# A fused GNN layer: the n gate summed in a PSUM bank that VectorE filled, and half of the edge scaling on VectorE

## The reference

```python
h = jnp.maximum(_layernorm(x), 0.0)
msg_input = jnp.concatenate([h[src], h[dst]], axis=1)
for t in range(4):
    m = jax.nn.relu(msg_input @ W1[t] + b1[t]) @ W2[t] + b2[t]
    msgs = msgs + jnp.where((edge_type == t)[:, None], m, 0)
agg = jax.ops.segment_sum(msgs, dst, num_segments=num_nodes)
gi = agg @ W_ih.T + b_ih                 # i_r, i_z, i_n
gh = h @ W_hh.T + b_hh                   # h_r, h_z, h_n
r = sigmoid(i_r + h_r); z = sigmoid(i_z + h_z)
n = tanh(i_n + r * h_n)
out = x + (1.0 - z) * n + z * h
```

## Time and profile before

| | |
|---|---|
| median of three runs | 1849.3 us (1848.07 to 1853.45) |
| span of the profiled execution | 1849.7 us |
| PE busy, weight loads | 1666.5 us (90%), 1413.8 us (76%) |
| VectorE busy | 1709.9 us (92%) |
| ScalarE busy | 1504.8 us (81%) |
| GpSimd busy | 1178.7 us (64%) |
| HBM traffic over the span | 172 GB/s |
| granted TensorE clock | 1.00 in all stretches of 200 us between 200 and 1600 us |

### The profile page before, as it was taken

One profiled execution on the slowest core, in us unless ns is written; L12 is line 12 of the kernel. 1 busy time (PEld: TensorE's weight loads), 2 busy tenths in 40 slices (PEclk: granted clock), 3 DMA queues, 4 the chain that ended last, 5 costly groups with the idle time before them and its releaser, 6 DMA issues.

```text
span 1849.7 us, 43490 instructions
## 1 busy us (share of the span) xinstructions
PE 1666.5 (90%) x10181; PEld 1413.8 (76%) x10181; DVE 1709.9 (92%) x4382; ACT 1504.8 (81%) x3401; POOL 1178.7 (64%) x1982
## 2 busy tenths in 40 slices
PE   0126899999999999999999999999999999999998
PEld 0125788888888888888888888888888888888786
DVE  8596799999999999999999999999999999999887
ACT  0025788898888888888889898889898889898895
POOL 4777776776776776767765656566566566666420
PEclk9999899999999999999999999999999999999999
DMA  2225677677777777777776776776767777776643
GB/s 69 51 51 139 171 191 195 186 193 191 192 185 192 189 193 185 185 192 187 188 187 190 187 190 181 193 186 187 185 191 183 190 183 191 186 189 185 174 137 94
DMA packets 477072, 319.73 MB, mean 173 GB/s; under 512 B 106705, under 2 KB 463009, under 8 KB 476962
## 3 DMA queue, kind: packets, MB, share of 16 engines
q10 hardware_dynamic: 261792, 156.12, 28.2%
q1 hardware_dynamic: 185730, 106.99, 25.1%
q0 software_dynamic: 29440, 55.47, 11.6%
HBM read 211.65 MB, written 106.72 MB: 172 GB/s over the span
## 4 chain that ended last, share of the span: by engine, by line
PE 55%; ACT 8%; issue 5%; ACTq 4%; DVE 1%; DVEq 0%
PE bank L1333 12%; PE bank L1335 9%; PE bank L1334 9%; PE bank L1413 8%; PE bank L1403 4%; PE bank L1395 4%; ACT n_zc L1288 3%; ACT n_h L1200 2%; PE bank L1425 2%; PE bank L1442 2%; PE bank L1424 2%; PE bank L1452 2%; ACTq L1217 2%; ACT e_r L1276 2%; ACTq L1238 2%
## 5 line engine op out<-in xcount | busy, mean ns | idle before, releaser
L581 POOL DMA_INDIRECT e_x<-in_x,rows_now x816 | 799.2, 979 | 243.3 <-issue 230.6
L1183 ACT ACTIVATE e_h<-e_x,shift,rstd 128x128 f32<-128x128 f32 x816 | 354.8, 490 | 93.7 <-DVE shift L1049 93.7
L1200 ACT ACTIVATE n_h<-n_x,shift,rstd 128x128 f32<-128x128 f32 x784 | 361.4, 488 | 2.2 <-issue 2.2
L1333 PE MATMUL bank<-n_h_hi,whh_hi 128*128 128x512 f32 x588 | 263.5, 448 | 37.5 <-ACT n_zc L1288 29.1
L1333 PE MATMUL bank<-n_a_hi,wih_hi 128*128 128x512 f32 x588 | 248.9, 423 | 0.0
L1072 DVE TENSOR_SCALAR n_sel<-iota,n_rel 128x256 fp32r<-128x256 f32 x784 | 237.3, 364 | 7.1 <-POOL n_rel L632 7.1
L1413 PE MATMUL bank<-n_sel,n_win 128*128 128x256 f32 x1568 | 234.9, 292 | 8.5 <-DVE n_sel L1072 8.3
L1335 PE MATMUL bank<-n_a_hi,wih_lo 128*128 128x512 f32 x588 | 232.3, 395 | 0.0
L1335 PE MATMUL bank<-n_h_hi,whh_lo 128*128 128x512 f32 x588 | 232.2, 395 | 0.0
L1334 PE MATMUL bank<-n_h_lo,whh_hi 128*128 128x512 f32 x588 | 232.0, 395 | 0.0
L1334 PE MATMUL bank<-n_a_lo,wih_hi 128*128 128x512 f32 x588 | 232.0, 394 | 0.0
(11 more groups left out here) (178 smaller groups left out, 4022.8 us busy)
## 6 DMA issues: line engine op xcount, KB each, us to landing
n_win<-messages SPq DMA_DIRECT2D x1568, 64.2 KB
messages<-e_msg ACTq DMA_DIRECT2D x204, 257.0 KB, 2.4
n_x<-in_x ACTq DMA_DIRECT2D x195, 256.0 KB
out<-n_out ACTq DMA_DIRECT2D x195, 256.0 KB
e_x<-in_x,rows_now POOLq DMA_INDIRECT x816
rows_now<-lists SPq DMA_DIRECT2D x204, 2.0 KB
lists<-picks,list_rows POOLq DMA_INDIRECT x72
w<-in_W SPq DMA_DIRECT2D x1, 512.0 KB, 4.8
```

Of the source, the lines that this page charges most:

```text
L581: G.indirect_dma_start(e_x[:, s, 2 * end + t, :], None, x, bass.IndirectOffsetOnAxis(ap=rows_now[:, s, t, end:end + 1], axis=0)).then_inc( ...
L1183: last = A.activation(e_h[:, s % 2, k, :], e_x[:, s, k, :], ACT.Relu, scale=rstd[:, slot, col + k:col + k + 1], bias=shift[:, slot, col + ...
L1200: last = A.activation(n_h[:, s % 2, cols], n_x[:, s, cols], ACT.Relu, scale=rstd[:, slot, col + 4 + k:col + 5 + k], bias=shift[:, slot, co ...
L1333: T.matmul(o, w_hi, v_hi, start=start, stop=False)
```

## The change

Four edits. VectorE's `(h_n + b) * r` is written into PSUM bank BIN instead of `n_t`, and PE's three products of the n gate add onto it, without clearing the bank first; so the products wait for n_ted, ScalarE's tanh reads the bank after n_gate_in, and the add of line 1105 with its semaphore is gone. One matmul ahead of the loop writes BIN once. VectorE makes tiles 2 and 3 of e_h (`scale_edges`, in the place of the add), as scale and shift without ReLU, and gives a new semaphore e_scaled. ScalarE makes tiles 0 and 1 with Relu as before, and its copy of the transposed tiles becomes a Relu. GpSimd waits for e_scaled wherever it waits for e_normed, and so does PE. ScalarE's order: n_h tile 0 goes ahead of sigmoid r, the tanh ahead of n_h tiles 1 and 2.

```diff
@@ -362,6 +362,7 @@
         n_stats = sem("n_stats")
         e_tagged = sem("e_tagged")
         e_normed = sem("e_normed")
+        e_scaled = sem("e_scaled")
         e_turned = sem("e_turned")
         e_evaced = sem("e_evaced")
         e_hid = sem("e_hid")
@@ -391,7 +392,6 @@
         n_red = sem("n_red")
         n_zed = sem("n_zed")
         n_ted = sem("n_ted")
-        n_ued = sem("n_ued")
         n_ned = sem("n_ned")
         n_ded = sem("n_ded")
         n_eed = sem("n_eed")
@@ -654,6 +654,7 @@
                         linked(G.tensor_tensor(new[:], root_t[:], old[:], ALU.mult))
                 if due(first - 4):
                     pool.wait_ge(e_normed, first - 4)
+                    pool.wait_ge(e_scaled, first - 4)
                 if due(first - LAG + 5):
                     pool.wait_ge(n_normed, first - LAG + 5)
                 G.tensor_tensor(rstd[:, slot, :], root_t[:], root[:], ALU.mult).then_inc(ln_rooted, 4)
@@ -670,6 +671,7 @@
                     pool.wait_ge(l_loaded[m % UNROLL], uses(i, m % UNROLL, UNROLL, 16))
                     if due(i - 7):
                         pool.wait_ge(e_normed, i - 7)
+                        pool.wait_ge(e_scaled, i - 7)
                 if h is not None:
                     wait_half(h)
                 transfers_may_start(i + 1 + 2 * TYPES)
@@ -1049,6 +1051,20 @@
                     V.scalar_tensor_tensor(out=shift[:, slot, :], in0=bn[:, slot, :, 1], scalar=-1.0, in1=rstd[:, slot, :],
                                            op0=ALU.mult, op1=ALU.mult).then_inc(ln_shifted, 4)
 
+            def scale_edges(i, m):
+
+                q, s, third = i - 7, (m - 7) % UNROLL, (m - 7) % 4
+                if not within(q, UNITS):
+                    return
+                dve.wait_ge(ln_shifted, q - third + 4)
+                if due(q - 1):
+                    dve.wait_ge(e_turned, q - 1)
+                for k in (2, 3):
+                    col = 8 * third + k
+                    last = V.tensor_scalar(e_h[:, s % 2, k, :], e_x[:, s, k, :], rstd[:, s // 4, col:col + 1],
+                                           shift[:, s // 4, col:col + 1], ALU.mult, ALU.add)
+                last.then_inc(e_scaled, 1)
+
             def step(i, m):
                 g, s = i - LAG - 2, (m - LAG - 2) % 4
                 if within(g, NG):
@@ -1079,9 +1095,9 @@
                 if within(g, NG):
                     dve.wait_ge(n_red, g + 1)
                     dve.wait_ge(n_gate_hn, g + 1)
-                    if due(g - 1):
-                        dve.wait_ge(n_ned, g - 1)
-                    V.scalar_tensor_tensor(out=n_t[:, s, :], in0=bank[BHN][:], scalar=bhh[:, 2:3], in1=n_r[:, s, :],
+                    if due(g):
+                        dve.wait_ge(n_ned, g)
+                    V.scalar_tensor_tensor(out=bank[BIN][:], in0=bank[BHN][:], scalar=bhh[:, 2:3], in1=n_r[:, s, :],
                                            op0=ALU.add, op1=ALU.mult).then_inc(n_ted, 1)
                 ln_part(i, m, 2)
                 g, s = i - LAG + 1, (m - LAG + 1) % UNROLL
@@ -1098,11 +1114,7 @@
                     dve.wait_ge(n_ahi, g + 1)
                     V.tensor_tensor(n_a_lo[:, s % 2, :], bank[BA][:], n_a_hi[:, s % 2, :].bitcast(F32),
                                     ALU.subtract).then_inc(n_alo, 1)
-                g, s = i - LAG, (m - LAG) % 2
-                if within(g, NG):
-                    dve.wait_ge(n_gate_in, g + 1)
-                    dve.wait_ge(n_ted, g + 1)
-                    V.tensor_tensor(n_t[:, s, :], bank[BIN][:], n_t[:, s, :], ALU.add).then_inc(n_ued, 1)
+                scale_edges(i, m)
                 if within(i - LAG + 8, NG):
                     last = node_stats(i - LAG + 8, m - LAG + 8, m - 1)
                 if last is not None:
@@ -1177,13 +1189,12 @@
                 if not within(q, UNITS):
                     return
                 slot, col = wait_norm(i, m)
-                if 0 in tiles and due(q - 1):
+                if due(q - 1):
                     act.wait_ge(e_turned, q - 1)
                 for k in tiles:
                     last = A.activation(e_h[:, s % 2, k, :], e_x[:, s, k, :], ACT.Relu,
                                         scale=rstd[:, slot, col + k:col + k + 1], bias=shift[:, slot, col + k:col + k + 1])
-                if 3 in tiles:
-                    last.then_inc(e_normed, 1)
+                last.then_inc(e_normed, 1)
 
             def normalise_nodes(i, m, tiles):
                 g, s = i - LAG + 2, (m - LAG + 2) % UNROLL
@@ -1239,21 +1250,21 @@
                                   n_out[:, s, :].rearrange("p (k d) -> p k d", k=TILES)).then_inc(n_stored[s], 16)
 
             def step(i, m):
-                normalise_edges(i, m, (0, 1, 2))
+                normalise_edges(i, m, (0, 1))
+                normalise_nodes(i, m, (0,))
                 g, s = i - LAG, (m - LAG) % 2
                 if within(g, NG):
                     act.wait_ge(n_gate_r, g + 1)
                     if due(g - 1):
                         act.wait_ge(n_ted, g - 1)
                     A.activation(n_r[:, s, :], bank[BRZ][:], ACT.Sigmoid, bias=bsum[:, 0:1]).then_inc(n_red, 1)
-                normalise_edges(i, m, (3,))
                 store_messages(i, m)
                 q, s = i - 8, (m - 8) % 2
                 if within(q, UNITS):
                     act.wait_ge(e_turned, q + 1)
                     if due(q - 1):
                         act.wait_ge(e_hid, q - 1)
-                    A.activation(e_ht[:, s, :], bank[BE0][:], ACT.Copy).then_inc(e_evaced, 1)
+                    A.activation(e_ht[:, s, :], bank[BE0][:], ACT.Relu).then_inc(e_evaced, 1)
                 g, s = i - LAG + 1, (m - LAG + 1) % 2
                 if within(g, NG):
                     act.wait_ge(n_turned, g + 1)
@@ -1262,7 +1273,6 @@
                     A.activation(n_h_hi[:, s, :], bank[BT[s]][:], ACT.Copy).then_inc(n_hhi, 1)
                     act.wait_ge(n_summed, g + 1)
                     A.activation(n_a_hi[:, s, :], bank[BA][:], ACT.Copy).then_inc(n_ahi, 1)
-                normalise_nodes(i, m, (0,))
                 store_out(i, m)
                 load_x(i, m)
                 q, s = i - 9, (m - 9) % 2
@@ -1275,13 +1285,14 @@
                         kind = 2 * ((m - 9) % 2) + t
                         last = A.activation(e_r[:, s, cols], bank[BE1][:, cols], ACT.Relu, bias=b1_cols[:, kind:kind + 1])
                     last.then_inc(e_relued, 1)
-                normalise_nodes(i, m, (1, 2))
                 g, s = i - LAG, (m - LAG) % 2
                 if within(g, NG):
-                    act.wait_ge(n_ued, g + 1)
+                    act.wait_ge(n_gate_in, g + 1)
                     if due(g - 1):
                         act.wait_ge(n_ded, g - 1)
-                    A.activation(n_n[:, s, :], n_t[:, s, :], ACT.Tanh, bias=bih[:, 2:3]).then_inc(n_ned, 1)
+                    A.activation(n_n[:, s, :], bank[BIN][:], ACT.Tanh, bias=bih[:, 2:3]).then_inc(n_ned, 1)
+                normalise_nodes(i, m, (1, 2))
+                if within(g, NG):
                     act.wait_ge(n_gate_z, g + 1)
                     if due(g - 1):
                         act.wait_ge(n_eed, g - 1)
@@ -1328,19 +1339,21 @@
                      ).then_inc(s_ranked, 1)
             pe.wait_ge(s_edges_ready, 1)
             pe.wait_ge(s_gates_ready, 1)
-
-            def product(o, w_hi, w_lo, v_hi, v_lo, start, stop):
-                T.matmul(o, w_hi, v_hi, start=start, stop=False)
-                T.matmul(o, w_hi, v_lo, start=False, stop=False)
-                return T.matmul(o, w_lo, v_hi, start=False, stop=stop)
-
-            def gate(b, row, s, sources):
+            T.matmul(bank[BIN][:], ones_r[:], b2_rows[:], start=True, stop=True)
+
+            def product(o, w_hi, w_lo, v_hi, v_lo, start, stop, onto):
+                start = start and not onto
+                T.matmul(o, w_hi, v_hi, start=start, stop=False, skip_group_check=onto)
+                T.matmul(o, w_hi, v_lo, start=False, stop=False, skip_group_check=onto)
+                return T.matmul(o, w_lo, v_hi, start=False, stop=stop, skip_group_check=onto)
+
+            def gate(b, row, s, sources, onto=False):
                 cols = slice(row * D, (row + 1) * D)
                 for n, source in enumerate(sources):
                     w_hi, w_lo, v_hi, v_lo = {"h": (whh_hi, whh_lo, n_h_hi, n_h_lo),
                                               "a": (wih_hi, wih_lo, n_a_hi, n_a_lo)}[source]
                     last = product(bank[b][:], w_hi[:, cols], w_lo[:, cols], v_hi[:, s, :], v_lo[:, s, :],
-                                   n == 0, n == len(sources) - 1)
+                                   n == 0, n == len(sources) - 1, onto)
                 return last
 
             def general_sums():
@@ -1389,6 +1402,7 @@
                 q, s = i - 8, (m - 8) % 2
                 if within(q, UNITS):
                     pe.wait_ge(e_normed, q + 1)
```

(6 more changed lines are left out.)

## The result

The changed kernel takes 1968.8 us (median of 4 runs, 1966.9 to 1969.8) against 1849.3 before, a ratio of 1.0635 with a 95% interval of 1.0619 to 1.0650. The forecast was slower, 1895 us, range 1868 to 1930: the direction and the mechanism hold, the size doesn't, +46 forecast and +119 measured. The profiled execution has a span of 1966.1 us and took 1968.0 in all.

A forecast was written before the change was run, and what follows sets the result against it. No engine alone: a tight PE and ScalarE ring in 8.43 us steps. Four steps, 33.7 us before, become 34.0 (quiet) or 35.6 (writing, with list writes): 1849.3 + 41 + 7 - 2 = 1895 us, range 1868 to 1930.

The forecast's parts named there:

- The moved release and the ring: GpSimd's gathers released 3.5 us later, closing n_sel, n_a_lo, scale, gate_word, n_rel, n_sel: 1895 us, chance 0.74.
- the ring keeps its slack: Rival: the release is still in time, so 0.2 us a step is gained: 1810 us, chance 0.09.
- gain and ring cancel: Rival: the ring costs only in fours with list writes, half of what was reckoned: about 1849 us, chance 0.05.
- the scalings hold up GpSimd: Rival: each scaling pair slows a GpSimd root instruction by 0.49 us, 33 in all: about 1927 us, chance 0.12.
- the rule that plain rounds are harmless: Ring turns without roots or list writes take 7.91 us, or 8.14 once in four, both below 8.2.
- The pair of scalings: VectorE's two 128-column scalings after n_a_lo: about 0.26 us each, ending 1.0 after n_a_lo starts (bounds 0.9 and 1.25).
- n_sel to n_a_lo: VectorE's stretch from n_sel's start to n_a_lo's start: 3.58 us, once in four steps 3.81.
- The release: From the end of VectorE's scalings to GpSimd's gate_word: 0.17 us.
- the root round: GpSimd's step with inverse roots: 10.04 us gate to gate, the 1.2 us seed wait gone; 17.95 for two steps.
- The head: First 19 steps, without n_sel and led by VectorE's list making: left as they are, no cost.
- The gain of the order: ScalarE's new order gains 0.2 us a step: 0.15 from n_h tile 0, 0.05 from the earlier tanh.
- The covered wait for n_ted: PE's n gate waits for VectorE's L1084, but earlier PE work covers it by about half a microsecond.

The follow-up runs named there:

- the wait alone: Kernel before plus one GpSimd wait ahead of the gathers, for VectorE's add of line 1105 in the step before; no work moved: 1983.5 us.
- n_rel first: n_rel put ahead of the first gather on GpSimd: 1818.6 us on the changed kernel, 1797.3 us on the changed kernel without scalings.
- the exchange: Kernel before, with n_rel moved ahead of the first gather on GpSimd: 1842.8 us.
- the gate half: Changed kernel without scalings or e_scaled: n gate summed in BIN, ScalarE's new order, all four e_h tiles on ScalarE: 1816.1 us.
- the fastest kernel: Changed kernel without scalings or e_scaled, all four e_h tiles on ScalarE, n_rel ahead of the first gather on GpSimd: 1797.3 us.

## Why the prediction was right in kind and wrong in size

*The moved release and the ring*: right. The two waits that it named are the two largest new ones, the wait alone reproduces the loss, and cutting the ring at n_rel gives 150 us back.

*The rival "the ring keeps its slack"*: excluded for the changed kernel; it is the state of the kernel before. *The rival "gain and ring cancel"*: excluded by +119. *The rival "the scalings hold up GpSimd"*: excluded by the trace. The root instructions of 0.59 and 0.64 us stand beside n_xh and n_e, which were there before. Those beside the scaling pair at 1129.88 took 0.25, like most; in the whole trace 94 root instructions ran beside a scaling and beside neither n_xh nor n_e, 0.25 in the median and 0.40 at most. It is the pair that got longer there, 0.72 instead of 0.59.

*The step that failed* is the sum's terms, each taken too low, and with them the rule that plain rounds are harmless. By the measured stretches: the 88 steps with list writes took 803.8 us instead of 742.0, +62, forecast 41; the 92 without 819.1 instead of 775.3, +44, forecast 7; the head 11, forecast 0; the tail 0, forecast -2. Together 117, and the spans differ by 116.4. Behind them:

- *The pair of scalings.* Forecast 0.18 apart and 0.26 long, ending 1.0 after n_a_lo starts. They are 0.255 apart and 0.335 long, ending at 1.19. I priced 128 columns between 32 and 256 columns; but these instructions, which read two scalars per partition, cost as much as n_sel's 256 columns with one. Whether the second scalar is the reason no run tells.
- *n_sel to n_a_lo.* Forecast 3.58, as in the first step of the earlier trace rows; it is 3.74. The four n_sel take 1.29 instead of 1.13: n_sel now nearly always starts 0.03 behind n_rel, so beside GpSimd's third gather, which itself takes 1.07 instead of 0.96. In the kernel before, n_sel met an idle GpSimd in most plain steps only: in the median (400 to 1600 us) it took 1.13 where i mod 4 is 3 or 0, but 1.28 and 1.32 where it is 1 and 2, and in the same order n_sel to n_a_lo was 3.58, 3.58, 3.73 and 3.87. Now it is 3.74, 3.74, 3.79 and 3.84: the plain turns, which the forecast held harmless, got nearly the whole increase. That the two meet because of the ring is shown; that the meeting is what lengthens them is inferred from the rows.
- *The release*, 0.22 instead of 0.17, and *the root round*, 10.5 instead of 10.04.
- *What these do together.* The plain turn shown is 8.29, not 7.91. The 0.4 falls on three turns of a quiet four, and 0.5 on the roots: 35.6 instead of 34.0. In a writing four two turns have it: 36.5 instead of 35.6. These 1.6 x 23 + 0.95 x 22 = 58 us are the larger part of the 71 that were missing. The bounds held the pair's price; what they left out is that all terms erred to the same side.
- *The head.* "I leave them as they are" was wrong: VectorE leads there, and twelve pairs of 0.51 are 6.1 us. n_sel of step 19 starts 6.7 us later, in each kernel with the pair by 5.9 us or more except the one with n_rel first; the exchange takes 2.4 off the head by itself (190.1 to 187.7), and the pair adds 6.8 there too (187.5 to 194.3). The other 4.5 us come in steps 19 to 22, where the ring is closed already: the wait alone adds 3.1 there.

*The gain of the order*: right in size, 0.2 forecast; the gate half's steps are 0.28 shorter without list writes and 0.08 with them, 0.26 to 0.29 with n_rel first. VectorE's lost add is in these numbers too; no run has it by itself. Its parts were ill divided: 0.10 for n_h tile 0 (0.15 forecast), about 0.1 for the tanh (0.05 forecast), both measured on the fastest kernel.

*The covered wait for n_ted*: right. It stands in the page's groups with 0.9 us in all.

```profile
L1346 PE MATMUL bank<-n_a_hi,wih_hi 128*128 128x512 f32 x588 | 249.6, 424 | 0.9 <-DVE bank L1100 0.9
```

*L1084 into PSUM*: 0.737 us as L1100 against 0.730, so nothing, as taken.

*The tensor_scalar rule of the Trainium skill* (VectorE: DVE Perf Modes, The perf-mode tier table) would have made the pair cheaper still; at 0.255 us for 128 columns this trace is further from it than n_sel was. The measurement decides.

## What to carry to other kernels

Before giving an instruction a later release, follow what stands behind the wait on the waiting engine, up to the instruction that the releasing engine itself needs next step: if the walk comes back, it is a ring, and its length, not any engine's load, is what must stay under the step. Price a ring's terms at their high ends, with its instructions running beside one another as the ring will make them, because a small error is paid turn after turn; and look for the cheap cut (here two statements exchanged on GpSimd, or one DMA issue moved on ScalarE) before moving work. Taking 163 us off ScalarE, which isn't in this ring, gave nothing.

## What was unexpected of the hardware

- A VectorE scale-and-shift of 128 fp32 columns with two per-partition scalars is followed by the next 0.255 us after its start (0.335 from start to end), as late as n_sel's 256 columns with one scalar (0.26).
- The four n_sel took 1.13 us when GpSimd was idle and 1.25 to 1.28 in the median beside its work, in the kernel before. Where an indirect DMA started 0.1 us behind them, they took 1.29 and the DMA 1.07 instead of 0.96: 166 times in the changed kernel, and 24 times in the gate half, where n_sel waits for n_rel in 18 steps only.
- A GpSimd instruction of 128x32 that takes 0.25 us took 0.74 in the median beside VectorE's n_xh or n_e, which read two SBUF tiles (48 times in the kernel before), but 0.25 beside a scaling, which reads one (94 times in the changed kernel).
- TensorE adds onto what VectorE wrote in a PSUM bank at no measurable price: the n gate's three matmuls are as long as before (0.424 us for the first, 0.423 before), VectorE's write takes 0.737 instead of 0.730, and the tanh reads the bank as it read SBUF (0.69 against 0.71 us).
